# Three moves in the prologue of a conditional residual kernel: a bias product spread among the mixture products, a weight load and its split put behind another operand's, and a context product put ahead of the attention's

## The reference, cut to what matters

```python
    def _L0_cond_ref(x, embedding, W0, b0, W1, b1, W2, b2, weight, bias_k):
        h = jax.nn.gelu(embedding @ W0 + b0, approximate=False)
        h = jax.nn.gelu(h @ W1 + b1, approximate=False)
        att = jax.nn.softmax((h @ W2 + b2) / T, axis=-1)
        agg_w = jnp.einsum('bk,koi->boi', att, weight[..., 0])
        agg_b = att @ bias_k
        out = jnp.einsum('boi,bih->boh', agg_w, x) + agg_b[:, :, None]
...
        out = lax.conv_general_dilated(x, weight, window_strides=(STRIDE,), padding=[(PAD, PAD)], dimension_numbers=('NCH', 'OIH', 'NCH'), feature_group_count=GROUPS)
        ctx = jnp.einsum('nd,od->no', c, c_weight)
        out = out + ctx[:, :, None] + bias[None, :, None]
...
    x = x + _L0_cond_ref(x, cond_128, ...)
    x = x + _L1_cond_ref(x, cond_128, L1_cond_weight, L1_cond_c_weight, fside_S_0)
    x = x + _L2_cond_ref(x, cond_128, ...)
    x = x + _L3_cond_ref(x, cond_128, ...)
```

## Time and profile before

| | us |
|---|---|
| median of 3 runs | 484.26 (484.23 to 484.34) |
| the profiled execution, its own time | 484.1 |
| its span on the core | 482.3 |
| PE busy | 473.2 (98%) |
| DVE busy | 320.2 (66%) |
| ACT busy | 248.5 (52%) |
| POOL busy | 151.2 (31%) |

### The profile page before, as it was taken

How to read it: one execution, slowest core, us unless ns; L and a number is a source line. 1 busy time by engine, 2 the same in 40 slices (tenths; PEclk the granted TensorE clock), 3 DMA queues, 4 the chain that set the end, 5 groups by cost and what they waited for, 6 DMA issues and landing times.

```text
span 482.3 us, 17714 instructions
## 1 busy us (share of the span) xinstructions
PE 473.2 (98%) x8003; PEld 446.3 (93%) x8003; DVE 320.2 (66%) x409; ACT 248.5 (52%) x414; POOL 151.2 (31%) x151
## 2 busy tenths in 40 slices
PE   8989999999999999999999999999999999999996
PEld 7978999999999999999999999999999999999995
DVE  3548687767676876767687776767777676777424
ACT  5654445466544545654455466444545654455544
POOL 2935072324133322414331331333223142420110
PEclk9999999999999999999999999999999999999998
DMA  8696977676546476664746666464667746452224
GB/s 277 207 334 184 302 232 226 209 221 208 186 120 215 156 217 219 207 216 112 211 149 217 209 214 216 129 206 140 215 203 220 220 149 208 131 187 77 90 88 175
DMA packets 39244, 92.86 MB, mean 193 GB/s; under 512 B 4601, under 2 KB 25473, under 8 KB 35201
## 3 DMA queue, kind: packets, MB, share of 16 engines
q1 hardware_dynamic: 39168, 91.73, 60.5%
HBM read 53.95 MB, written 37.77 MB: 190 GB/s over the span
## 4 chain that ended last, share of the span: by engine, by line
PE 97%; DMA 1%; issue 1%; DVE 0%; SPq 0%; DVEq 0%
PE cv_ps L508 59%; PE aux_ps L488 18%; PE aux_ps L537 15%; PE cv_ps L444 2%; PE cv_ps L431 1%; DMA consts_sb<-in_consts_dram 1%; PE cv_ps L537 1%; PE aux_ps L431 1%; PE aux_ps L466 0%; DVE y_all L847 0%; DVE m_all L797 0%; PE aux_ps L455 0%; PE aux_ps L400 0%; SPq L318 0%; SPq L319 0%
## 5 line engine op out<-in xcount | busy, mean ns | idle before, releaser
L508 PE MATMUL cv_ps<-x_hi,conv_lo 32*128 32x512 f32 x1536 | 284.7, 391 | 0.0
L508 PE MATMUL cv_ps<-x_hi,conv_hi 32*128 32x512 f32 x1536 | 284.2, 389 | 0.0
L508 PE MATMUL cv_ps<-x_lo,conv_hi 32*128 32x512 f32 x1536 | 284.2, 391 | 0.0
L508 PEld LDWEIGHTS cv_ps<-x_lo,conv_hi 32*128 32x128 f32 x1536 | 172.5, 184 | 4.7
L508 PEld LDWEIGHTS cv_ps<-x_hi,conv_hi 32*128 32x128 f32 x1536 | 171.5, 183 | 5.6
L508 PEld LDWEIGHTS cv_ps<-x_hi,conv_lo 32*128 32x128 f32 x1536 | 172.4, 183 | 4.5
L779 DVE SCALAR_TENSOR_TENSOR x_lo<-cv_ps,d_all,x_hi 128x512 fp32r<-128x512 f32 x128 | 87.2, 744 | 132.4 <-ACT x_hi L626 132.4
L636 ACT ACTIVATE y_all<-aux_ps,e_all 128x512 f32<-128x512 f32 x122 | 74.0, 689 | 134.1 <-PE aux_ps L537 134.1
L626 ACT ACTIVATE x_hi<-cv_ps,d_all 128x512 fp32r<-128x512 f32 x128 | 77.5, 688 | 67.9 <-PE cv_ps L508 67.9
L488 PE MATMUL aux_ps<-x_hi,a_hi 32*128 32x512 f32 x512 | 99.5, 391 | 2.3 <-issue 2.3
L488 PE MATMUL aux_ps<-x_hi,a_lo 32*128 32x512 f32 x512 | 99.1, 388 | 0.0
(11 more groups left out here) (104 smaller groups left out, 455.5 us busy)
## 6 DMA issues: line engine op xcount, KB each, us to landing
x_sb<-in_x_dram SPq DMA_DIRECT2D x31, 1024.0 KB, 6.5
out_dram<-y_all SPq DMA_DIRECT2D x60, 512.0 KB, 7.4
a_rep<-a_pairs SPq DMA_DIRECT2D x64, 128.0 KB, 7.3
m_rep<-m_pairs SPq DMA_DIRECT2D x64, 128.0 KB, 6.1
out_dram<-y_all SPq DMA_DIRECT2D x8, 256.0 KB, 2.6
a_pairs<-a_all SPq DMA_DIRECT2D x1, 1920.0 KB, 12.4
m_pairs<-m_all SPq DMA_DIRECT2D x1, 1792.0 KB, 12.2
m_all<-in_mix_dram SPq DMA_DIRECT2D x2, 512.0 KB, 5.5
```

The costliest lines, as they stand in the source:

```text
L508: mm = pe.matmul(cv_ps[:, g, :], w[rows(g), j, :], a[n % 2][rows(g), q, s:s + T], start=(i == 0), stop=(i == steps - 1))
```

## The change

Three things move; no product, load or split is added or removed.

- `bias_e` becomes a fifth generator beside the four mixture lanes. It lets four rounds pass (`E_BEHIND`), then gives one product a round to the end of round 12 + 4 = 16 and on to round 25. Before, it stood as two blocks: six products behind round 19 and four behind the last round.
- On SP the load of `conv_f` moves behind the save of a0's first pair and ahead of `replicate_a0(0)`. On POOL `split_a0(0)` moves between the identity and the split of the convolution's weights.
- `bias_d` moves from between L400 and L403 to the front of `attention`.

```diff
-            sp.dma_start(conv_f[:], conv).then_inc(conv_loaded, DMA)
             sp.wait_ge(d_ready, 1)
             sp.dma_start(d_dram, d_sb[:]).then_inc(d_saved, DMA)
...
             save(a0_all, a0_dram, 0, 1, a0_saved[0])
+            sp.dma_start(conv_f[:], conv).then_inc(conv_loaded, DMA)
             replicate_a0(0, range(PH))
...
-                bias_d()
...
-            def bias_e(options):
-                if 0 in options:
-                    pe.wait_ge(e_loaded, DMA)
-                    pe.wait_ge(c2_att_ready, 1)
-                    for n in range(1, NL):
-                        pe.matmul(e_ps, bias_sb[:, n, :], att_t[:, n, :], start=(n == 1), stop=False)
-                for k in options:
+            def bias_e():
+
+                for _ in range(E_BEHIND):
+                    yield
+                pe.wait_ge(e_loaded, DMA)
+                pe.wait_ge(c2_att_ready, 1)
+                for n in range(1, NL):
+                    pe.matmul(e_ps, bias_sb[:, n, :], att_t[:, n, :], start=(n == 1), stop=False)
+                    yield
+                for k in range(K):
                     mm = pe.matmul(e_ps, w3_sb[:, k, :], c2_att[:, k, :], start=False, stop=(k == K - 1))
-                return mm
+                    if k == K - 1:
+                        mm.then_inc(e_made, 1)
+                    yield
...
             fill(8)
+            bias_d()
             attention()
...
             in_turn(mixing, 3 * G)
             biases()
-            in_turn(mixing, 2 * G)
-            bias_e(range(0, 4))
-            in_turn(mixing)
-            bias_e(range(4, K)).then_inc(e_made, 1)
+            in_turn([*mixing, bias_e()])
...
+            split_a0(0)
             pool.wait_ge(pool_chain, PH)
             nc.gpsimd.tensor_copy(conv_hi[:], conv_f[:]).then_inc(conv_split, 1)
             pool.wait_ge(conv_split, 1)
             nc.gpsimd.tensor_tensor(conv_lo[:], conv_f[:], conv_hi[:].bitcast(F32), ALU.subtract).then_inc(conv_split, 1)
-            split_a0(0)
             split_a0(1)
```

More of the change, by code:

```diff
@@ L37 @@
 QUAD = 4
+E_BEHIND = 4
 REPEAT = 4
```

## The result

The changed kernel takes 488.46 us, median of seven executions (487.01 to 490.7), against 484.23 for the kernel before (seven: 484.04 to 485.7): a ratio of 1.0086, with a 95% interval of 1.0062 to 1.0111. It is slower by 4.2 us. 483.0 was forecast, and 484.5 was the upper end of the range. The profiled execution took 487.46, with a span of 485.7 where before it was 482.3. It is 1.0 short of the median, so it shows a milder case of what follows.

A forecast was written before the change was run, and what follows sets the result against it. TensorE was taken as the bound, 473.2 of 482.3 us busy, leaving one 2.3 us wait to win. Gain 2.26 less loss 1.00 made 1.26 us: 483.0 against 484.26, range 482.1 to 484.5.

The forecast's parts named there:

- A round is then 0.60: Mixture rounds 18 to 25, each with a pair of 128-row bias passes: 0.60 us each, quads at 21.26, loss 1.00.
- The way out: Switch from 128-row passes back to row groups within a mixture round: taken at 0.21 us.
- the way in: Switch from row groups to the 128-row passes within a mixture round: taken at 0.16 us.
- the rival's 0.77: Full drain at both switches: 0.77 us a round, quads at 22.65, loss 2.39, 484.4 us; chance 0.13.
- the gain of 2.26: TensorE's wait for a0 before layer 0 of sample 0, 24.10 to 26.36, goes: 2.26 us won.
- R: Time the last of the four a0 reads lands: 20.4 forecast, 2.0 earlier than before; bounds 20.0 and 22.4.
- the rival of 0.15: Reads of a0 not earlier (R near 22.4), or x's split shares with POOL: say 483.9 us; chance 0.15.
- the one of 0.07: Convolution weights land late, after 18.48, moving all POOL work; with 11.1 us again, 485.7 us; chance 0.07.
- the signs by which the forecast said that it would be wrong: conv_f landing after 19, a0_rep landing after 21.5, or a change in TensorE's steady part.
- The last evacuations stand bare: Before the quads, the second bias block no longer covers DVE's last evacuations, 0.69 us; part of the 1.00 loss.
- This cap: Lane 3 of layer 0, sample 1: TensorE at most 1.9 us ahead if DVE and POOL take turns, 0.9 if sharing.
- The third move: Context product placed ahead of the attention, in the softmax wait: zero, bounded by one pass of 0.1 either way.

The follow-up runs named there:

- bias_32rows: The changed kernel with the eight bias products reading 32 of their 128 rows, so none needs the whole array: 485.29 us, ratio 1.0025.
- load_ctx: The changed kernel without the spreading of the bias (load, splits and context product moved): 485.43 us, ratio 1.0022 against the kernel before.
- pool_only_fill: pool_only with five more idle products before the softmax, thirteen in place of eight: 484.91 us, ratio 1.0008 against the kernel before.
- bias_alone: The kernel before with only the bias products spread among the mixtures, loads and splits as before: 490.47 us, ratio 1.0134.
- bias_pairs: The kernel before with the bias spread, but the eight 128-row products two at a time in four rounds: 486.61 us, ratio 1.0037.
- bias_filled: bias_alone with three idle products of 128 columns ahead of each of the eight products: 493.89 us, ratio 1.0172 against the kernel before.
- load_alone: The kernel before with only the convolution weights' load behind a0's save and a0's split ahead of the weights' split: 485.64 us, ratio 1.0019.
- before_fill: The kernel before with thirteen idle products, not eight, before the softmax and 14 more ahead of layer 0: 484.35 us, ratio 0.9996.
- before_again: The kernel before, unchanged, profiled once more: 485.83 us, span 484.0.
- hi_first: The kernel before with a0's split for sample 0 between the high and low parts of the convolution's weights on POOL: 483.76 us, ratio 0.9990.
- behind_reads: The kernel before with the convolution weights' load behind the four a0 reads, and a0's split ahead of POOL's weight work: 484.31 us, ratio 1.0008.
- pool_only: The kernel before with only POOL's order changed, a0's split for sample 0 ahead of the weights' split: 484.43 us, ratio 0.9999.

## Why the prediction was wrong

The forecast had the quads at 21.26 and, at 3.84 for them, layer 0 of sample 0 at 25.10; in the profiled execution these are 23.16 and 29.75. So it was off by 1.90 before the quads and by 2.75 in them, 4.65 together; its time was off by 4.62 (487.46 against 482.84). Two terms of the sum failed.

**The first step that failed: "A round is then 0.60".** It is 0.77, 1.4 us over eight rounds. The term that is wrong is not the one that the forecast doubted. The way out, taken at 0.21, is 0.21. The lanes' second passes were put at 0.11 behind their first, the spacing of steady rounds, and come at 0.21 behind a switch; the way in from the last start is 0.20, where 0.16 was taken from a start rounded to 19.0; and the second wide pass comes at 0.13, not 0.114. The profile of the kernel before had all of these. Of the 0.5 that is left to the quads, 0.2 is that the mixtures began at 9.55 and not 9.34, and 0.1 that TensorE started 0.14 behind the evacuation, where 0.05 was taken; 0.2 isn't traced.

That the rival's 0.77 (0.11 + 0.27 + 0.114 + 0.28, a full drain both ways) is the measured number is in part luck: its parts give 0.38 for the row groups and 0.39 for the wide pair, and the trace has 0.43 and 0.34. The rule it came from (the Trainium skill, TensorEngine Tiling (Array Packing), "Key Properties": a change of tiling mode drains TensorE) was given 0.13. The trace agrees with it as far as every switch costs time, and doesn't show whether the drain is complete. `bias_32rows` ties the loss to the whole-array products, by its median.

**The second step that failed, and the larger one: the clock was put at nothing.** The sum takes the quads at 3.84, their length at full clock, without a reason why the clock should hold behind the rounds, and its worst case for the bias was a loss of 2.4 against the gain of 2.26. The granted clock falls to 0.50 for 6.8 us, which puts 2.75 on the quads alone. It goes with the spreading: in all four profiles of kernels that have it, a stretch at 0.50 begins at 21.0 to 27.7 (here 22.2). Of the ten others three have none on record ahead of the kernel's end, five have one from 9.2 to 9.7 on, one at 27.5 and one at 34.8. Three of the four also started slowly, but so did `load_ctx` and `pool_only_fill`, without a fall between 21.0 and 27.7. All seven executions of the changed kernel have a mean clock of 0.993 or less, and one of ten of `load_ctx` and two of ten of `bias_32rows`, whose medians are 3 us lower. Why such rounds are followed by it stays open. `bias_alone` has it begin inside the rounds, `bias_pairs` 3 us behind them, and `bias_filled`, with more work in each round, didn't prevent it.

**Right, but with the wrong size: R and the weights.** The save landed 1.7 us after issue, even sooner than the 2.4 taken. The 768 KB, taken at 4.5, needed 6.9, and held up the reads behind it: R 23.1 and not 20.4, the rival of 0.15, and the weights at 20.98 and not 18.4, the condition of the one of 0.07. These are two of the signs by which the forecast said that it would be wrong, though neither made the loss: a0 was ready at 25.07, before even the 26.36 of the kernel before. In `load_alone` they cost 1.0019 with an interval that holds 1, because a0 of sample 0, ready at 25.3 there, is still ahead of the old 26.25; what they delay is sample 1, by 0.5.

**Right.** The wait of 2.26 is gone. The last evacuations stand bare (0.9 of waiting). DVE's subtraction and POOL's long one take turns: 4.01 in `load_alone` for 1.22 alone, ending 1.1 behind POOL's (the Trainium skill, SBUF — State Buffer, "Who interferes with whom", makes the shared port pair an exclusive lock; the trace agrees). This cap didn't come to decide anything. The third move is nothing (`load_ctx` beside `load_alone`). The steady part of TensorE didn't change.

**The wait that was to be won may be partly in use.** Of the 23 executions of the kernel before beside `before_fill`, five have a mean clock of 1.000 and take 483.82 to 484.21; seven have 0.990 to 0.995 and take 483.83 to 484.55; six more have 0.986 to 0.996 and take 485.3 to 486.0. One reading is that a low stretch costs next to nothing there as long as it comes before the wait, and 1.5 us when it comes behind it. Only the second half is seen (`before_again`); no profile of the kernel before has a stretch ahead of the wait. `hi_first` fits the reading from the other side: the wait is gone, the quads start 1.26 late behind a low stretch, and of 2.26 us only 1.0 is won. `behind_reads`, `load_alone`, `pool_only` and `hi_first` have the best executions of all (482.7 to 483.2) and most of them a wide spread, and no median that can be told from 484.3. The mean clock doesn't explain all of that spread: single executions at 0.998 and 0.999 took 485.4 and 484.5. A part may be slow starts, which the mean clock leaves out: the profiled execution of `load_ctx`, at 0.998 and 485.74, has one (see the last section).

## What to carry to other kernels

Don't put single whole-array products among products of row groups to fill a gap: each costs a switch there and back (here rounds of 0.77 us in place of 0.22, for 0.23 us of work), and behind eight in a row the clock was down. Keep them in blocks. To price a switch, read the whole round behind one in the trace, not the spacings of steady rounds around it: here the second pass behind a switch came at 0.21, where the sum took the 0.11 of steady rounds. Before counting a removed wait as gain, look at what its length takes in, such as executions in which earlier work is slow. A sum of lengths at full clock needs its own case for a clock that falls. And a large load moved ahead of small reads in one queue is paid by the reads, even when the queue is otherwise nearly empty.

## What the runs showed of the hardware

- TensorE's granted clock fell to 0.50 in or behind rounds that switch between row groups and the whole array (6.8 us in the changed kernel, 10.2 in `bias_alone`, 3.4 in `bias_pairs` and `bias_filled`), and behind a wait of about 2.2 us before layer 0 (3.4 us in `before_again`). It also fell at 9.2 to 9.7, about the start of the mixtures behind the softmax, in five profiles: for 3.4 us in `load_alone`, `behind_reads`, `pool_only` and `hi_first`, and for 23.9 us in the profiled execution of `bias_32rows`. `before_fill`, with products in both waits, shows no mean clock under 0.997 in twelve executions.
- TensorE can also be slow at its start where the profile's clock reads 1.00. Eight idle products took 1.22 us in most profiled executions and 2.08 in `bias_alone`, `bias_pairs`, `bias_filled` and `load_ctx`; in these four the first 24 mixture passes took 1.8 us too, where the kernel before took 0.97. That is about what they take at a recorded 0.50 (1.8 in `pool_only`). In these profiles the clock's record begins only at 14.0 to 14.8, so the 1.00 ahead of it says that nothing is recorded, and the mean clock leaves the slow start out. In `bias_alone`:

```profile
6.76 2.08 PE L411 MATMUL cv_ps<-idle_sb 128*128 128x256 f32 x8
```

```profile
7.00:8.00 1.00, 1.00 (x6) 1.00 (x7) 0.74 (x4) 0.99 (x3) 0.00 (x0) 1.00 0.91 357
```

- A 128 KB save to DRAM landed in 1.7 us in a queue that was nearly done and in 4.4 behind a backlog; reads of 128 KB took 2.2 to 4.7 us, and 3.9 to 6.3 behind 768 KB.
